# Two cross-attention passes rewritten: one fp32 exponential, stationary values in 32-column tiles, the maximum written out by GpSimd

## The reference, cut to what matters

```
q = heads(x @ Wq + bq);  k = heads(ctx @ Wk + bk);  v = heads(ctx @ Wv + bv)
scores = einsum('bhqd,bhkd->bhqk', q, k) / sqrt(8)
scores = where(mask, -1e18, scores)                 # first pass only
out = softmax(scores) @ v, heads side by side, @ Wo + bo
x = layernorm(x + out)
```

## Time and profile before

| what | value |
|---|---|
| median of 3 runs | 1996.22 us (1986.47 to 1997.43) |
| the profiled execution's own time | 2002.27 us |
| its span, 38458 instructions | 2000.5 us |
| mean granted TensorE clock | 0.824 |
| busy: PE, PEld (weight loads) | 1325.9, 983.8 us |
| busy: DVE (VectorE), ACT (ScalarE), POOL (GpSimd) | 1157.7, 894.5, 887.3 us |

### The profile page before, as it was taken

The page is one execution under the profiler, slowest core; times in us unless marked ns, Lnnn a source line. Parts: engine busy times, 40 slices in busy tenths (PEclk is TensorE's granted clock), DMA queues, the critical chain, the costliest instruction groups (busy, mean ns, idle before and its releaser), DMA issues. The chain is left out here.

```text
span 2000.5 us, 38458 instructions
## 1 busy us (share of the span) xinstructions
PE 1325.9 (66%) x13213; PEld 983.8 (49%) x13332; DVE 1157.7 (58%) x2836; ACT 894.5 (45%) x2497; POOL 887.3 (44%) x1026
## 2 busy tenths in 40 slices
PE   5999999999938888884423888005267777751460
PEld 2666666667714555553312787005145555540360
DVE  6666666665337887885721454345456766627244
ACT  2666666666725666662201333004156666623220
POOL 4666666656332222223373000761345666643316
PEclk9999999999968998996556999557578888865685
DMA  4221222111021112102411222222211111044222
GB/s 173 82 74 71 77 74 79 68 68 63 7 61 31 31 30 51 32 19 84 146 72 52 65 70 57 58 65 75 68 35 29 29 50 29 20 144 141 65 64 74
DMA packets 181617, 129.37 MB, mean 65 GB/s; under 512 B 57267, under 2 KB 151901, under 8 KB 181300
## 3 DMA queue, kind: packets, MB, share of 16 engines
q1 hardware_dynamic: 175284, 114.69, 18.8%
q0 software_dynamic: 6144, 12.22, 2.0%
HBM read 51.68 MB, written 33.55 MB: 43 GB/s over the span
## 5 line engine op out<-in xcount | busy, mean ns | idle before, releaser
L1124 POOL TENSOR_TENSOR own_pn<-own_p,own_recip 128x512 f32<-128x512 f32 x128 | 133.0, 1039 | 185.8 <-DVE own_recip L1173 185.8
L1619 POOL DMA_INDIRECT mix_got<-results,mix_fetch x96 | 95.2, 991 | 266.3 <-DMA results<-mix_yo 239.0
L741 DVE TENSOR_REDUCE cross_negmax<-cross_scores 128x4 f32<-128x512 f32 x256 | 173.8, 679 | 37.0 <-PE cross_scores L449 36.6
L265 POOL TENSOR_TENSOR cross_pl<-cross_pf,cross_ph 128x512 f16<-128x512 f32 x128 | 147.5, 1155 | 89.8 <-ACT cross_pf L576 89.4
L1083 ACT ACTIVATE own_p<-own_scores,own_negmax 128x128 f32<-128x128 f32 x512 | 181.7, 374 | 5.2 <-DVE own_negmax L1179 5.2
L575 ACT ACTIVATE cross_ph<-cross_scoresT 128x512 f16<-128x512 f32 x256 | 152.8, 597 | 64.1 <-PE cross_scoresT L491 54.2
L489 PE MATMUL cross_scoresT<-cross_qk,cross_kblock 128*128 128x128 f16 x1024 | 162.6, 238 | 3.9 <-issue 1.1
L491 PE MATMUL cross_scoresT<-cross_maxT,cross_sel 128*128 128x128 bf16 x1024 | 162.2, 238 | 0.0
L978 PE MATMUL own_scores<-own_k,own_q 64*128 64x128 f32 x1024 | 147.9, 285 | 12.3 <-issue 6.5
L576 ACT ACTIVATE cross_pf<-cross_scoresT 128x512 f32<-128x512 f32 x256 | 152.7, 597 | 0.0
L1076 ACT COPY own_pt<-own_turned 128x512 f32<-128x512 f32 x128 | 74.9, 585 | 168.9 <-PE own_turned L987 168.9
(11 more groups left out here) (283 smaller groups left out, 4348.1 us busy)
## 6 DMA issues: line engine op xcount, KB each, us to landing
own_swapped<-own_crossed SPq DMA_DIRECT2D x256, 128.0 KB, 2.0
mix_stage<-in_mix_w SPq DMA_DIRECT2D x48, 256.0 KB, 4.2
cross_kblock<-cross_krows SPq DMA_DIRECT2D x64, 128.0 KB, 3.3
slots<-mix_blank SPq DMA_DIRECT2D x14, 512.0 KB, 6.1
mix_xg<-slots SPq DMA_DIRECT2D x56, 128.0 KB, 2.3
results<-mix_yo SPq DMA_DIRECT2D x56, 128.0 KB, 1.8
cross_xin<-after SPq DMA_DIRECT2D x16, 256.0 KB, 3.2
cross_cin<-in_ctx SPq DMA_DIRECT2D x16, 256.0 KB, 3.5
```

What stands on the lines that cost most here:

```text
L265: ops.tensor_tensor(pl[g][:], pf[g % 2][:], ph[g][:], ALU.subtract).then_inc(s_plow, 1)
L741: nc.vector.tensor_reduce(negmax[bb % 2][:, HU * seat(g):HU * seat(g) + HU], scp[g % 2][:].rearrange("p (h t) -> p h t", h=HU), AX.X, ALU. ...
L1124: nc.gpsimd.tensor_tensor(pn[i][:], p[i][:], recip[i][:].unsqueeze(2).to_broadcast([P, HU, P]), ALU.mult)\
```

## The change

`attention_pass` is replaced by `cross_attention_pass`, without the self-attention branch, and both cross passes call it. Slots run from -18 to 133 with one unit a slot; a row's later steps follow at fixed distances (4 to 9 slots). What it does in a unit:

```diff
 # PE
-  mask on scoresT, 4 x (scoresT; selector x maxT), 12 fp16 matmuls of 128x9
+  def scores_turned(u):
+      pe.wait_ge(s_less, u + 1); wait(pe, s_exp, u - 1)
+      for j in range(HU):
+          o = stp[u % 2][:, j * P:(j + 1) * P]
+          nc.tensor.matmul(o, less[u % NB][:, j, :], identb[:], start=True, stop=False, ...)
+          mm = nc.tensor.matmul(o, kblock[n % 2][:, g, b, j, :], q[n % 2][:, g, b * S:(b + 1) * S], ...)
+  def attend(u):                       # v is fp32, 128 x 32: 8 values, a one, 23 zeros
+      pe.wait_ge(s_exp, u + 1)
+      if g == 0: wait(pe, s_ev, row)
+      for j in range(HU):
+          mm = nc.tensor.matmul(avp[W * j:W * j + W, g * P:(g + 1) * P], v[n % 2][:, b, 4 * g + j, :],
+                                pt[u % 3][:, j * P:(j + 1) * P], start=True, stop=True, ...)
+  def turn_back(row):                  # once a row
+      pe.wait_ge(s_ev, row + 1); wait(pe, s_y, row)
+      for g in range(UNITS):
+          mm = nc.tensor.transpose(msc[:, g * P:(g + 1) * P], turned[row % 2][:, g * P:(g + 1) * P], ident[:])
 # ACT
-  nc.scalar.activation(ph[g][:], stp[g % 2][:], ACT.Exp, scale=scale)
-  nc.scalar.activation(pf[g % 2][:], stp[g % 2][:], ACT.Exp, scale=scale).then_inc(s_exp, 1)
+  nc.scalar.activation(pt[u % 3][:], stp[u % 2][:], ACT.Exp, scale=scale).then_inc(s_exp, 1)
+  def attended(row):                   # once a row
+      nc.scalar.copy(turned[row % 2][:], avp[:]).then_inc(s_ev, 1)
 # POOL
-  max parts in bf16, once a row; pl in the unmasked pass
+  def less_max(u):
+      pool.wait_ge(s_max, u + 1); wait(pool, s_ST, u - NB + 1)
+      shift = negmax[u % NB][:].unsqueeze(2).to_broadcast([P, HU, P])
+      if masked:
+          ins = nc.gpsimd.tensor_tensor(less[u % NB][:], addmask[...].unsqueeze(1).to_broadcast([P, HU, P]), shift, ALU.add)
+      else:
+          ins = nc.gpsimd.tensor_copy(less[u % NB][:], shift)      # less is bf16, 128 x 512
 # DVE
-  pl in the masked pass; vl (v's low part)
```

The order on TensorE in slot t, and the opening:

```diff
+  for t in range(FIRST, LAST + 3):
+      if row_at(t, 2) is not None: attend(t - 2)
+      if 0 <= t + LA < NU: scores(t + LA)                  # LA = 3
+      if t in slot_items: item(*slot_items[t])
+      if 0 <= t < NU: scores_turned(t)
+      if 0 <= t - 1 < NU and (t - 1) % UNITS: attend(t - 1)
+      for late, step in ((5, turn_back), (6, turn_att), (7, out)): ...
+  ITEMS = ("ctxT", "k0", "k1", "k2", "k3", "xT", "q0", "q1", "q2", "q3", "v")
+  ITEM_SLOT = (-18, -17, -16, -14, -13, -11, -10, -8, -7, -5, -4)
+  # SP, after each k item: the spread of that unit's keys, 16 DMAs a quad instead of 4
+  for j in range(HU):
+      sp.dma_start(kblock[n % 2][32 * j:32 * j + 32, g, :, j, :], krows[32 * j:32 * j + 32, g])
+  # POOL at the start, twice: kblock, v's zeros, v's ones
+  nc.gpsimd.memset(kblock[i][:]...); nc.gpsimd.memset(v[i][:, :, :, DH + 1:W], 0.0); nc.gpsimd.memset(v[i][:, :, :, DH:DH + 1], 1.0)
```

More of the change, by code:

```diff
@@ L109, in attention_pass @@
[L109 to L118, removed]
-            qk = [sb(f"qk{i}", [P, NC, QUAD * S], F16) for i in range(2)]
-            krows = sb("krows", [P, NC, QUAD, S], F16)
-            kblock = [sb(f"kblock{i}", [P, NC, QUAD, HU, S], F16) for i in range(2)]
@@ L267, in hold_late @@
-        def hold_late(eng, s, value, held):
-            if not (isinstance(value, int) and value <= 0):
-                hold(eng, s, value, held)
-        def place(g, j):
-            return 64 * (g % 2), 64, 4 * (g // 2) + j
-        def seat(g):
-            return 2 * (g % 2) + g // 2 if own else g
         block = ctx.enter_context(nc.Block())
@@ new lines, in _ @@
+            split("k")
+            for t in range(FIRST, LAST + 4):
+                row = row_at(t, 7)
+                if row is not None:
+                    att_high(row)
+                if t in slot_items:
+                    item(*slot_items[t])
+                if t == FIRST:
+                    for a in ("q", "v", "o"):
+                        split(a)
+                if 0 <= t < NU:
+                    exp(t)
+                row = row_at(t, 4)
+                if row is not None:
+                    attended(row)
@@ new lines, in _ @@
+            pool.wait_ge(s_late, 16 * 4)
+            for t in range(FIRST, LAST + 4):
+                if t in slot_items:
+                    n, m = slot_items[t]
+                    if ITEMS[m] == "xT" and masked:
+                        mask(n)
+                    if ITEMS[m] == "q3":
+                        residual(n)
+                row = row_at(t, 8)
+                if row is not None:
+                    root(row)
+                if 0 <= t + LA - 1 < NU:
+                    less_max(t + LA - 1)
@@ new lines, in norm @@
+            def norm(row):
+                dve.wait_ge(s_rstd, 2 * row + 2)
+                wait(dve, s_out[row % NXO], 16 * (row // NXO))
+                nc.vector.tensor_scalar(xout[row % NXO][:, 0, :], ysum[row % 2][:], mv[row % 2][:, 0:1], rstd[:],
+                                        ALU.subtract, ALU.mult).then_inc(s_ln, 1)
+            dve.wait_ge(s_const, 16 * 2)
+            for a in range(2):
+                ins = nc.vector.tensor_scalar(low_bias[:, a, :], bias[:, a, :], low_rows[:, a:a + 1], None, ALU.mult)
```

971 lines of the change are left out of this document (347 added, 624 removed).

## The result

The changed kernel takes 1836.54 us (median of four runs, 1829.1 to 1841.74) against 1996.83 of the kernel before in the same comparison: a ratio of 0.920, 95% interval 0.916 to 0.924, or 160 us less. The forecast was 1863, 134 us less, with 1815 to 1895 as its own range.

The account below looks back on a forecast made before the run. The prediction took chains of waits (`attend` on the division and `pl`) to bound the unmasked pass, with no engine full in either. Pace -47.5 and -54.1, openings -34, ends +2 sum to -133.6 us: 1863 us, range 1815 to 1895.

Parts of the forecast that it names:

- Pace: Time per unit in the cross passes: masked 2.454 to 2.08 us, unmasked 2.356 to 1.93, with TensorE at 95% and 91%.
- The 26 us of the earlier trace: Unmasked pass before: `attend` waits 13.2 us per 100 for the division and 13.1 for `pl`; both were to fall away.
- the pace times 127 steps: Fall in pace applied uniformly between first and last exponential of each cross pass: -47.5 us masked, -54.1 unmasked.
- the 0.42 of the items: TensorE's price in us a unit for the quad's items (projections, transposes), 6.7 us per quad, in both versions.
- The block: Four fp32 attends in 32-column tiles on TensorE: 0.45 us a unit, two switches of tile shape at 0.16 together included.
- VectorE, ScalarE, GpSimd: Loads of the other engines in the masked pass: 1.59, about 1.2 and 1.69 us a unit.
- The opening: Start of each cross pass to its first exponential: 33 us against 50.2, 17 less in each pass.
- the ends: Last row of each cross pass adds an evicting copy and the transposes back: +1 us a pass.
- More gaps: Rival: new order keeps TensorE at 85%, or `less_max` costs 1.785; paces 2.26 to 2.3 and 2.0 to 2.1, about 1905 us; chance 0.25.
- Tiles in series: Rival: column tiles do not overlap, block 1.04 us, 2022 us in all; slower where the block exceeds about 0.9; chance 0.06.
- The kept chain: Rival: the in-order chain still sets the pace, 2.48 and 2.73 us a unit, 2015 us in all; chance 0.09.
- GpSimd: Rival: a `less_max` on GpSimd takes above 2.2 us, so the kernel ends slower; chance 0.02.

Follow-up runs that it names:

- x_same: Changed kernel with a unit's four heads all written to the same 32-column tile, so the attends no longer run side by side: 1962.28 us, ratio 0.982.
- x_statp: Changed kernel with the probabilities stationary again, in fp32, nine value columns moving, no column tiles and no turn back of the row: 1918.17 us, ratio 0.958.
- x_pl: Changed kernel with a second, 16-bit exponential and its difference computed again (VectorE in the masked pass, GpSimd in the unmasked), neither read: 1929.6 us, ratio 0.966.
- x_first: Changed kernel with VectorE's steps of the attended rows (division, low part, sum, norm) ahead of the reduction of the scores in every slot: 1814.65 us, ratio 0.910.
- x_nomask: Changed kernel without the mask matmul on the scores whose maximum VectorE takes, in the masked pass; one 512-column matmul a unit less: 1821.3 us, ratio 0.911.
- y_quad: y_order with a row's four attends issued in one block: 1772.07 us, ratio 0.888.
- y_order: Changed kernel with x_first's VectorE order, x_open's opening, and the turns of context and x one slot earlier: 1791.91 us, ratio 0.898.
- x_open: Changed kernel with another opening: GpSimd's second key zeroing later, first key spread and output-bias wait relaxed, two small VectorE operations moved to ScalarE: 1825.24 us, ratio 0.914.

## Why the prediction was right

**Pace.** Forecast 2.08 and 1.93, measured 2.08 and 1.93 in the middle quads, with TensorE at 96 and 93 busy (forecast 95 and 91) and the clock at 1.00. x_same shows the price of the block at work, x_statp what stationary probabilities in fp32 would cost (the kernel before had them in fp16, 0.31 a unit by the earlier trace rows). Three things in the reasons did not hold as they stood. The 26 us of the earlier trace rows count one wait twice: what went in the unmasked pass is 13.2 us for the division, with `pl` ready only 0.2 to 0.6 us earlier. In the masked pass neither wait was large, so that 85 would become 95 was a likeness to the self attention and not a wait that goes; x_pl shows there that VectorE without `pl` is needed. And the 91% was given to VectorE's load, while x_first makes VectorE busier and the pace shorter: its order it was, so that this figure fits by luck. x_nomask limits the claim further: TensorE's issue was the bound for about half of a change in it.

**The term that was mis-sized** is the pace times 127 steps. The first quad has no finished rows behind it and the last ones run out of projections: 31.3, five times 33.3, 32.0 and 26.3 us (15 steps) in the masked pass, 28.7, five times 30.8, 29.3 and 23.2 in the other. The steps fell by 55.8 and 64.0 us, forecast 47.5 and 54.1: 18 of the 26 us by which the two passes beat the sum. I had the 0.42 of the items in the price of every unit, the last 15 included, which have none. I also took a pace of middle quads (2.08) from one that averages over all (2.454); against 2.54, the fall in pace is 0.46 and not 0.374.

**The block** was taken at 0.45 and takes 0.45, from two wrong parts. Four tiles overlap whole: in y_quad's block 32 records take 1.11, and its tiles' records come in fours 0.109 apart, so one unit's two fours are 0.22 and the switches 0.23, not 0.16. The Trainium skill (TensorE: Matmul & The Clock Gate, on packing small matmuls) has the overlap as measured here; the estimate of 0.39 that I worked out with it was low by the switches. That a change of tiling mode drains the engine, as the Trainium skill has it (TensorEngine Tiling (Array Packing), Tiling Modes), fits the cost of the switches: without three of four pairs of them the pace fell by 0.113 and 0.071 from y_order to y_quad, of 0.17 freed.

**VectorE, ScalarE, GpSimd.** Forecast 1.59, 1.2 and 1.69 us a unit in the masked pass; 78.23, 57.50 and 65.95 per 100 at 2.08 are 1.63, 1.20 and 1.37. `less_max` took 1.038, below the 1.155 of the earlier trace rows. In the unmasked pass I put GpSimd near 1.5; its copy takes 0.613, and it is at 0.84. `xout` was to take 1 us in both; it takes 0.86 and 0.49. Neither was on the path.

**The opening** came to 30.8 and 30.6, forecast 33, and went through the steps in the order that was forecast, 2 to 3 us sooner from the first on: both `low_bias`, and Wk's split and the context's low part behind them, got through at the first memset's end. k1 is done 11.4 us into the pass (forecast 14.4), k3 15.3 (18), q3 25.2 (27.5). The timeline of the opening after:

```profile
555.85 6.92 POOL L392 MEMSET cross_kblock<- 128x8192 f16 x1 [3.19 <-POOLq L43]
...
560.65 2.16 DVE L507 TENSOR_SCALAR cross_low_bias<-cross_bias,cross_low_rows 128x4 f32<-128x4 f32 x2 [7.60 <-DMA cross_low_rows<-in_c_low_rows]
...
564.10 6.94 POOL L392 MEMSET cross_kblock<- 128x8192 f16 x1
...
567.22 0.28 DVE L447 TENSOR_TENSOR cross_wol<-cross_stage_o,cross_woh 128x128 f16<-128x128 f32 x1
567.41 3.71 DVE L525 COPY cross_vbias_b<-cross_vbias 128x128 f32<-128x128 f32 x1
...
571.07 11.62 SPq L193 DMA_DIRECT2D cross_kblock<-cross_krows  x16
```

The `low_bias` end at 562.81, 7.0 us into the pass, where 8.4 was forecast for the second. The stall of `vbias_b` behind the second memset ends 15.3 us in (forecast 15.7), and the spread runs from 15.2 to 26.8 (forecast 15.7 to 27). x_open, which takes the stall away among other things, opens 3.7 and 4.2 us sooner: that the stall itself lay on the path is likely and not shown. The openings are 5 us of the 26, and the ends, forecast at +1 each and measured at +0.3 and -1.3, the last 3.

**The rivals.** More gaps: TensorE's use rose, it did not stay at 85. Tiles in series: x_same is that kernel, and it is still faster than before (1962), so this rival was priced 60 us too high, and its turning point of 0.9 for the block too low (1.09 here). An estimated 38 of the 60 are gaps that it took as they are in the new order and that fill (middle paces 2.59 and 2.39, priced 2.69 and 2.58); most of the rest is again the uniform pace. The kept chain: the wait for the one attended bank is gone, and neither pace is near its 2.48 and 2.73. GpSimd: 66 and 44 busy per 100.

## What to carry to other kernels

Price a pass by stretches with the same work: the first and last turns of a software pipeline carry less, and a uniform pace overstates them; subtract like from like, middle from middle. Before two waits are added, see whether they are the same stretch of time. When the busiest engine loses work, look at once for the step that its order makes late, for here nearly half of a freed matmul, and most of the freed switches, went into waits; the switches' time came back when the queue of an engine with room stood in another order (for the matmul that was not tried). On an engine that executes in order, put the operation that others wait for ahead of one that itself still waits and has slack.

## What was not expected of the hardware

- TensorE's clock fell to 0.50 in the last quads of x_statp, behind a stretch of fp32 matmuls with nine moving columns, while its records still showed it 100 busy (870 to 890 and 1670 to 1690 us). By the ratio of last to middle quad in the changed kernel (26.3 to 33.3 and 23.2 to 30.8), those quads should have taken some 29 and 25 us: an estimated 31 us of its loss go with the clock.
- GpSimd's memset held a copy of VectorE for 3.71 us, while a subtraction of two tiles in SBUF ran through it in 0.28 (the fence above). The Trainium skill (SBUF — State Buffer, Who interferes with whom) states both: copies and scalar operations can take the port pair that GpSimd shares, and an operation with two inputs in SBUF contends only where GpSimd reads. The trace agrees on the memset, which reads nothing. On reads it agrees in part: in x_pl's masked pass the subtraction `pl` takes 0.69 us where GpSimd does nothing and 1.21 on average beside `less_max` alone, but in the kernel before it takes 0.68 beside GpSimd's `xres` too (seven times), which reads two tiles in SBUF.
